# Two MLP weights repacked in HBM, so that each load reads one contiguous run per partition

## The reference

```python
xn = _layernorm(x)
s = attention_block(xn)   # linear attention, then an MLP, both with residuals
g = _silu(slot_ffn(xn))   # routes every token to 8 of 64 slots, updates the slots, mixes them back
x = x + s * g
```

```python
x = q_x + attn
h = _ln(x, ln2_w, ln2_b)
h = jax.nn.gelu(h @ fc_w + fc_b, approximate=False)
return x + (h @ proj_w + proj_b)
```

## Time and profile before

| | |
|---|---|
| two runs | 2377.13 and 2430.29 us, median 2403.71 us |
| the profiled execution | 2390.99 us |
| its slowest core (core 4), span | 2389.4 us |
| spans of the 8 cores | 2342.8 to 2389.4 us |
| TensorE busy | 1214.5 us (51% of the span) |
| VectorE, ScalarE, GpSimd busy | 22%, 21%, 5% |
| DMA packets | 341,425, of which 305,171 are under 512 bytes |
| queue of the DMAs that POOL issues | 182,144 packets, 72.72 MB, 26.7% of the 16 engines' span |

### The profile page before, as it was taken

How to read it: one execution, slowest core, us unless ns; L and a number is a source line. 1 busy time by engine, 2 the same in 40 slices (tenths; PEclk the granted TensorE clock), 3 DMA queues, 4 the chain that set the end, 5 groups by cost and what they waited for, 6 DMA issues and landing times. The chain is left out here.

```text
span 2389.4 us, 18749 instructions; the slowest of 8 cores (2342.8 to 2389.4 us)
## 1 busy us (share of the span) xinstructions
PE 1214.5 (51%) x6220; PEld 569.0 (24%) x6308; DVE 533.9 (22%) x1213; ACT 502.7 (21%) x748; POOL 122.5 (5%) x139
## 2 busy tenths in 40 slices
PE   0143454544424321825726636540098598597696
PEld 0021222222211100312312222220043243243242
DVE  0223233323300112233223223220400400301102
ACT  0144444344410100200100101100230430421521
POOL 1000000000001001000000000003101001001000
PEclk9976766776766555957958858765599799799798
DMA  7511011011058324431331431619909809629356
GB/s 130 105 51 71 36 71 71 36 71 70 1 77 130 59 40 75 93 67 53 97 78 50 107 56 58 119 36 154 164 1 86 161 1 106 141 23 107 83 51 90
DMA packets 341425, 183.65 MB, mean 77 GB/s; under 512 B 305171, under 2 KB 309396, under 8 KB 341332
## 3 DMA queue, kind: packets, MB, share of 16 engines
q0 software_dynamic: 182144, 72.72, 26.7%
q1 hardware_dynamic: 159188, 109.74, 16.2%
HBM read 204.81 MB, written 33.56 MB: 100 GB/s over the span
## 5 line engine op out<-in xcount | busy, mean ns | idle before, releaser
L683 PE MATMUL pM<-xnTs,w1ab 128*128 128x512 bf16 x496 | 143.0, 453 | 50.6 <-ACTq L192 50.0
L669 PE MATMUL pT<-cIDb,xnb 128*128 128x128 bf16 x256 | 31.9, 303 | 242.3 <-ACTq L192 156.4
L1944 DVE TENSOR_TENSOR y1t<-pTf,y1t 128x512 f32<-128x512 f32 x32 | 22.1, 692 | 527.1 <-PE pTf L2038 527.1
L2007 PE MATMUL pMa<-h2T,fcwb 128*128 128x512 bf16 x496 | 125.5, 393 | 21.6 <-ACTq L192 20.9
L2024 PE MATMUL pPb<-g1F,pjcb 128*128 128x512 bf16 x504 | 119.0, 394 | 10.3 <-DMA pjcb<-pjw 9.9
L2007 PE MATMUL pMb<-h2T,fcwb 128*128 128x512 bf16 x504 | 123.2, 387 | 0.4
L2024 PE MATMUL pPa<-g1F,pjcb 128*128 128x512 bf16 x500 | 114.4, 385 | 10.6 <-DMA pjcb<-pjw 5.2
L1604 ACT ACT_TABLE_LOAD x4 | 5.1, 1283 | 505.4 <-PE pBig L1557 505.4
L517 DVE BATCH_NORM_STATS2 ST<-xld 128x6 f32<-128x512 f32 x64 | 43.6, 681 | 280.4 <-ACTq L192 279.8
L1991 PE MATMUL pT0d<-cIDb,h2b 128*128 128x128 bf16 x128 | 16.2, 306 | 158.1 <-DVEq L192 97.7
L683 PEld LDWEIGHTS pM<-xnTs,w1ab 128*128 128x128 bf16 x512 | 56.0, 113 | 134.0 <-issue 100.2
(11 more groups left out here) (263 smaller groups left out, 1768.4 us busy)
## 6 DMA issues: line engine op xcount, KB each, us to landing
xld<-x8k SPq DMA_DIRECT2D x64, 512.0 KB, 5.6
pjcb<-pjw POOLq DMA_DIRECT2D x32, 1024.0 KB, 11.0
scr_qk<-tmb SPq DMA_DIRECT2D x16, 512.0 KB, 2.6
y1scr<-XN SPq DMA_DIRECT2D x4, 2048.0 KB, 7.1
y1t<-y1scr SPq DMA_DIRECT2D x4, 2048.0 KB, 10.2
fcwb<-fcw POOLq DMA_DIRECT2D x32, 256.0 KB, 19.2
xre<-x8k SPq DMA_DIRECT2D x16, 512.0 KB, 11.3
out<-xre SPq DMA_DIRECT2D x16, 512.0 KB, 4.1
```

Source lines behind the costliest of these rows:

```text
L669: i = t.transpose(dstb[:, cc * 128:(cc + 1) * 128], xb[:, cc * 128:(cc + 1) * 128], cIDb[:])
L683: i = t.matmul(dstp[:, 0:512], w1ab[:, cc * 512 + ch * 128: cc * 512 + (ch + 1) * 128], xnTs[:, cc * 512:(cc + 1) * 512], start=(cc == 0), ...
L1944: i = v.tensor_tensor(y1v(mt).rearrange("p (s w) -> p s w", s=4)[:, :, d * 128:(d + 1) * 128], pTf[:, :].rearrange("p (s w) -> p s w", s=4 ...
L2007: i = t.matmul(dstp[:, :], fcwb[:, m * 1024 + cc * 128: m * 1024 + (cc + 1) * 128], h2T[:, cc * 512:(cc + 1) * 512], start=(cc == 0), stop ...
```

## The change

The host now stores both weights in HBM in the order in which SBUF holds them, one row of 32768 float32 (128 KB) per partition. `load_fc` then copies 1024 contiguous float32 per partition in each of its 8 DMAs, and `load_pj` 4096. The loops, the waits, the counts of the semaphores, the number of DMAs and what lies in `fcwb` and `pjcb` afterwards stay as they are. The instructions of all engines stand in the same order as before; only the shapes of these 64 DMAs differ, on POOL: 128x1024 in place of 128x8x128 for `fcwb`, 128x4096 in place of 128x32x128 for `pjcb`. Within a quarter, DMA k now brings all 8 input chunks of output chunk m = 8q + k, where DMA cc brought input chunk cc of all 8 output chunks.

```diff
-        "wo": g("attn_wo"), "fcw": g("attn_fc_w"), "pjw": g("attn_proj_w"),
+        "wo": g("attn_wo"),
+        "fcw": np.ascontiguousarray(
+            g("attn_fc_w").reshape(8, 128, 4, 8, 128)
+            .transpose(1, 2, 3, 0, 4).reshape(128, 32768)),
+        "pjw": np.ascontiguousarray(
+            g("attn_proj_w").reshape(32, 128, 8, 128)
+            .transpose(1, 2, 0, 3).reshape(128, 32768)),
...
-    wo_d = di("wo", [D, D]); fcw_d = di("fcw", [D, MLP]); pjw_d = di("pjw", [MLP, D])
+    wo_d = di("wo", [D, D])
+    fcw_d = di("fcw", [128, 32768]); pjw_d = di("pjw", [128, 32768])
...
                 def load_fc(eng, q):
-                    for cc in range(8):
-                        srcap = bass.AP(fcw_d.tensor,
-                                        cc * 128 * 4096 + q * 1024,
-                                        [[4096, 128], [128, 8], [1, 128]])
-                        dstap = bass.AP(fcwb, q * 8 * 1024 + cc * 128,
-                                        [[32768, 128], [1024, 8], [1, 128]])
-                        eng.dma_start(out=dstap,
+                    for k in range(8):
+                        col = q * 8192 + k * 1024
+                        srcap = bass.AP(fcw_d.tensor, col,
+                                        [[32768, 128], [1, 1024]])
+                        eng.dma_start(out=fcwb[:, col:col + 1024],
                                       in_=srcap).then_inc(sfc[q % 2], 16)
...
             def load_pj(g, dout, slot):
-                srcap = bass.AP(pjw_d.tensor, dout * 128,
-                                [[1024, 128], [128 * 1024, 32], [1, 128]])
-                dstap = pjcb[:, slot * 4096:(slot + 1) * 4096].rearrange(
-                    "p (m w) -> p m w", m=32)
-                g.dma_start(out=dstap, in_=srcap).then_inc(spj[slot], 16)
+                srcap = bass.AP(pjw_d.tensor, dout * 4096,
+                                [[32768, 128], [1, 4096]])
+                g.dma_start(out=pjcb[:, slot * 4096:(slot + 1) * 4096],
+                            in_=srcap).then_inc(spj[slot], 16)
```

## The result

The changed kernel takes 2354.24 us (median of 11 runs, 2350.77 to 2477.71) against 2394.06 us for the kernel before (10 runs, 2377.13 to 2431.99). The ratio is 0.985, with a 95% interval of 0.983 to 0.988: 1.5% faster, 35 us. The profiled execution took 2344.05 us, and its slowest core is now core 0 with 2342.5 us.

What follows compares the result with a forecast made beforehand. It took the kernel to be bound by the `fcwb` transfer in its block, then by late `pjcb` loads, with TensorE bounding the rest. 2391.0 - 16 - 25 = 2350 us, range 2325 to 2384.

Steps and rivals of the forecast that it cites:

- the likeliest case: Whole kernel: time within 2% of the profiled 2391.0 us, chance 0.70.
- both terms: The two gains summed: 16 us from the block loading `fcwb`, 25 us from the product with `pjcb`.
- The block lasts until its DMAs have landed: Block loading `fcwb`: a block where POOL issues DMAs ends some 0.6 us after they have landed.
- The block's length of 59.7 us: Block loading `fcwb`, after the change: 59.7 us, taken as the middle of 54.6 and 65.0.
- The price per MB from `wqb`, `wkb` and `wvb`: Loads at the kernel's start: 4 MB in long runs take 3.42 or 2.84 us per MB, applied to `fcwb`.
- the 3.45 us that I charged for the start and the end: Block loading `fcwb`: 2.85 us as the fixed part of a load plus 0.6 us from landing to block end.
- The block's gain of 16 us: Block loading `fcwb`: shrinks from 75.7 to 59.7 us, 16 us less (10.7 to 21.1).
- The landing of 8.1 to 8.9 us: `pjcb` loads: land in 8.1 to 8.9 us, 10.4 with the slowest start, against a budget of 9.44.
- The phases: Four token tiles' products with `pjcb`: 67.4 us each without waits, 28 us to be had, 25 taken.
- Half-clock groups go with the waits: Product with `pjcb`: groups at TensorE's lower clock follow long waits and vanish with them, counted within the 28 us.
- The base of the sum: Whole kernel: gains subtracted from the profiled execution's 2391.0 us, not the median shown, 2403.7 us.
- The pitch as a rival: Both loads: rows 128 KB apart halve the rate; block 34 us longer, `pjcb` phases 68 us more, 2493 us; chance 0.05.

Runs made afterwards that it cites:

- run 35: Not a label of a run: from run to run, 35 us were gained, with medians of 2394.06 us before and 2354.24 us for the changed kernel.
- the contiguous variant: Against the changed kernel, the 128 runs of each DMA lie one behind the other in HBM, not 128 KB apart; ratio 0.982 to the kernel before.

## Why the prediction was right, and where it was off

The forecast was 2350 us; 2354.2 were measured, within the range of 2325 to 2384, and with a ratio of 0.985 the time is within 2% of the one before, as the likeliest case had it. The gain is further off than the time: 41 us were forecast, 35 came, and both terms were too large, by 4 and by 3 us. The mechanism is the one that was forecast, in both places.

- **The block lasts until its DMAs have landed.** Right, and shown by moving the loads out of it (80.2 and 68.5 us of idle time become 18.7 and 21.3).
- **The block's length of 59.7 us.** Core 4 came to 60.6, the mean of the cores to 60.5, the range to 58.9 to 62.3. The price per MB from `wqb`, `wkb` and `wvb` carried over the earlier trace rows. (The middle of 54.6 and 65.0 is 59.8, and the 0.6 us that I had charged for the block's end were 1.8.) About 358 GB/s per core, which the Trainium skill (HBM Reference, "Specifications (TRN2)") gives for paired cores and by which an estimate of the transfer alone is 53 us, agrees: 60.5 less the 3.45 us that I charged for the start and the end leaves 57 us for 18.9 million bytes, 331 GB/s, 8% below the page.
- **The block's gain of 16 us.** 11.7 in the mean; on core 4 it was 15.0. The step that was off is taking the block before from core 4's profile, 75.7 us: the mean was 72.2, and core 7 had 69.0. The transfer after was sized rightly, the one before was the longest of eight.
- **The landing of 8.1 to 8.9 us.** 8.2 in the mean, with core medians of 7.5 to 8.8. Interpolating between a small load and a price per MB was good enough to decide a question of 1 us.
- **The phases.** 67.4 us without waits were worked out, 67.6 to 67.8 measured. I had taken 25 us of the 28, for loads with a slow start. There were no such waits, but the mean core had less to win than core 4: 22.2 us, where core 4 won 27.2 (from 690.8 to 663.6). The two deviations nearly cancel, and that the term came within 3 us is luck.
- **Half-clock groups go with the waits.** Right. Before, 30 groups on the eight cores took over 7.2 us, each of them right behind a wait for `pjcb`, and together cost 6.7 us per core over 7.07; after, there is none. It does not go the other way round: 117 groups had waited, so 87 waits, one of 2.0 us among them, were followed by a group at full clock, while one of 0.7 us was not. The time between the groups of a phase is 15.0 us shorter per core, 12.0 of it the listed waits; with the 6.7 that is 21.7 of the 22.2 us.
- **The base of the sum.** The sum went from the profiled execution, 2391.0 us, whose slowest core was the last into the block, had the longest block and nearly the longest waits. From profile to profile the kernel gained 47 us, from run to run 35.
- **The pitch as a rival.** For runs of 4 and 16 KB it fell: the contiguous variant is faster by 0.5 us in the block and not in the landing. By the Trainium skill's rule (DMA: Bandwidth & Descriptors, "Latency and other measured facts"), which is for copies within HBM, I had estimated a loss of 3% or less at this pitch, and 60.5 against 60.0 us does not contradict that. What I had put down for this rival was a misreading. 4.7 us per MB in the `fcwb` block left out the 2 MB of `y1t` and the fixed part; with both, 75.7 less 3.45 us for 18 MB is 4.0 us per MB, no slower than the 4.3 of a `pjcb` load.

## What to carry to other kernels

A block or barrier on the engine that issues DMAs can end with the landing and not with the issue; compare the last issue, the landing and the first instruction behind it, and move loads whose data are needed later out of such a block before making them faster. For loads in a double-buffered loop, work out the time from the release of the slot to the next use of it: a load that misses it by 1 us can pay again in TensorE's clock, as 30 of 117 groups did here, and one that meets it is worth nothing more. When a DMA is cut into short pieces, look at both of its sides, for either can be what cuts it. And take both stretches from every core: the slowest core's profile overstated one term by over a third.

## What the runs showed that I had not expected

- Runs of 512 bytes read from rows 128 KB apart were slower than the same runs in the arrays of before: 11.5 against 10.6 us for 2 MB read, and 0.9% of the whole kernel. Whether it is the pitch of the rows stays open. Runs of 4 KB lost nothing that shows, 60.5 against 60.0 us in the block, and neither did those of 16 KB, 8.2 against 8.5 us to landing.
- POOL's issue takes longer with more runs: 0.53 us for 128, 0.92 for 1,024, 1.67 for 4,096.
- In the block before, POOL stopped after 15, 23 and 31 loads, though the waits in the code stand ahead of loads 17 and 25 only; the last issue came 9.35 us after the one ahead of it. With runs of 4 KB it stops after 16 and 24, as the code says. What held it is not shown, nor whether it cost the block anything.
- Faster loads can delay the load beside them: with the loads of `fcwb` in the second block, VectorE was idle for 21.3 us ahead of the last part beside long runs and for 18.7 beside short ones.
